# Attention scores through the leaky slope first: one exponential a graph with its row sum on ScalarE, in a four-stage graph and mixture kernel

## What is computed

```python
x = x + _L0_gnn_ref(_layernorm(x), adj, ...)      # slope 0.2,  elu at the end
x = x + _L0_ffn_ref(_layernorm(x), ...)           # 8 experts, the best two of each node
x = x + _L1_gnn_ref(_layernorm(x), adj, ...)      # slope 0.01, relu at the end
x = x + _L1_ffn_ref(_layernorm(x), ...)           # 32 experts, the best one

h = x @ W
s1, s2 = h @ a1, h @ a2
e = leaky_relu(s1[:, :, None] + s2[:, None, :], negative_slope=alpha)
attention = softmax(where(adj > 0, e, NEG_BIG), axis=-1)
h_prime = attention @ h
```

## Time and profile before

| | us |
|---|---|
| median of 3 runs | 1112.64 (1110.25 to 1114.04) |
| the profiled execution | 1112.51 |
| its span | 1110.8 |
| mean granted TensorE clock | 0.879 |

### The profile page before, as it was taken

How to read it: one execution, slowest core, us unless ns; L and a number is a source line. 1 busy time by engine, 2 the same in 40 slices (tenths; PEclk the granted TensorE clock), 3 DMA queues, 4 the chain that set the end, 5 groups by cost and what they waited for, 6 DMA issues and landing times. The chain is left out here.

```text
span 1110.8 us, 26952 instructions
## 1 busy us (share of the span) xinstructions
PE 888.1 (80%) x6709; PEld 799.2 (72%) x6709; DVE 788.0 (71%) x3507; ACT 699.1 (63%) x2364; POOL 765.7 (69%) x983
## 2 busy tenths in 40 slices
PE   5988898888619999999999669999999418888720
PEld 4777787777509999999999658888888406666620
DVE  7688989898848999999999617888888713322310
ACT  3998988898405655656656369999998216643300
POOL 4347767777753888887788801778787846777776
PEclk9998989898659999999999979999999659976655
DMA  9333442221167888877878221222221135433301
GB/s 213 69 96 118 135 133 60 64 73 33 40 141 201 210 212 211 206 210 209 207 206 208 66 68 39 79 79 79 79 81 51 53 96 145 116 99 105 93 31 38
DMA packets 144904, 129.21 MB, mean 116 GB/s; under 512 B 26521, under 2 KB 116510, under 8 KB 144754
## 3 DMA queue, kind: packets, MB, share of 16 engines
q1 hardware_dynamic: 124114, 91.94, 33.4%
q0 software_dynamic: 17760, 34.20, 9.1%
q10 hardware_dynamic: 2880, 1.35, 0.6%
HBM read 82.74 MB, written 47.48 MB: 117 GB/s over the span
## 5 line engine op out<-in xcount | busy, mean ns | idle before, releaser
L505 POOL DMA_INDIRECT xs<-staged,dst x256 | 258.8, 1011 | 77.0 <-issue 68.5
L1172 ACT ACTIVATE hT<-bank,wt 128x128 f32<-128x128 f32 x620 | 177.3, 368 | 131.3 <-PE bank L1392 115.3
L551 POOL DMA_INDIRECT x2d<-ob,xi x155 | 161.3, 1040 | 41.6 <-issue 27.3
L573 POOL DMA_INDIRECT out<-oq,xq x144 | 142.8, 991 | 58.2 <-issue 42.7
L1378 PE MATMUL bank<-xnT,wt 128*128 128x128 f32 x1240 | 165.8, 277 | 0.0
L1392 PE MATMUL bank<-w2s,hT 128*128 x1240 | 164.1, 275 | 0.6 <-DVE ob L1044 0.5
L1378 PEld LDWEIGHTS bank<-xnT,wt 128*128 128x128 f32 x1240 | 152.6, 194 | 0.1
L1392 PEld LDWEIGHTS bank<-w2s,hT 128*128 128x128 f32 x1240 | 150.9, 192 | 1.0 <-issue 1.0
L1121 ACT ACTIVATE p<-bank,nm 128x128 f32<-128x128 f32 x256 | 103.1, 403 | 19.6 <-DVE nm L746 19.6
L1122 ACT ACTIVATE p<-bank,nm 128x128 f32<-128x128 f32 x256 | 104.8, 410 | 0.0
L1135 ACT ACTIVATE rl<-bank,rinv 128x128 f32<-128x128 f32 x256 | 97.1, 453 | 3.1 <-DVE staged L738 3.1
(11 more groups left out here) (249 smaller groups left out, 2202.6 us busy)
## 6 DMA issues: line engine op xcount, KB each, us to landing
wt<-wpd SPq DMA_DIRECT2D x155, 258.0 KB
xi<-xs SPq DMA_DIRECT2D x155, 66.0 KB
xq<-xs SPq DMA_DIRECT2D x144, 66.0 KB
xb<-x2d SPq DMA_DIRECT2D x32, 258.0 KB, 3.2
xb<-in_x SPq DMA_DIRECT2D x32, 256.0 KB, 3.2
wpd<-w1c SPq DMA_DIRECT2D x56, 129.0 KB, 3.3
xs<-staged,dst POOLq DMA_INDIRECT x256, 2.6
x2d<-ob,xi POOLq DMA_INDIRECT x155
```

The lines of the kernel that those rows point to most:

```text
L505: pool.indirect_dma_start(out=xs[l], out_offset=bass.IndirectOffsetOnAxis(ap=dst[b % ND][:, c:c + 1], axis=0), in_=stag[s][:, q, 0:ROW], i ...
L551: pool.indirect_dma_start(out=x2d, out_offset=bass.IndirectOffsetOnAxis(ap=xi[t % NXI][:, ID:ID + 1].bitcast(U32), axis=0), in_=ob[:, t % ...
L573: pool.indirect_dma_start(out=orow, out_offset=bass.IndirectOffsetOnAxis(ap=xq[j % NXQ][:, q, ID:ID + 1].bitcast(U32), axis=0), in_=oq[j % ...
L1172: last = act.activation(hT[t % 2][:, j, :], HID[t % 2][:, j, :], ACT.Gelu, bias=wt[t % NW][:, c:c + 1])
```

## The change

The score is put through the leaky slope before the exponential: S + min(S, 0)(slope - 1). In layer 1 VectorE does it, with a tensor_scalar from PSUM into `leaky` and an add. In layer 0 ScalarE forms relu((slope - 1) S), which is min(S, 0)(slope - 1), into `leaky` (event `below`), and VectorE adds S. The row maximum with its sign turned is then `nm` itself. ScalarE takes one exponential a graph from `leaky`, with `accum_out` for the row sum. `pm`, `nm`, `rsum` and `leaky` have two buffers each. TensorE now waits for `leaky` of group m-2 before it forms scores, and for `exps` before the transpose of `pm`; the moments' parts stand in a row ahead of the reciprocal.

```diff
             def weights(n, moments=()):
+                for part in moments:
+                    part()
                 after(dve, "exps", n)
-                after(dve, "pt_ps", n - 1)
                 after(dve, "er", n - 3)
-                for q in range(G):
-                    last = dve.scalar_tensor_tensor(pm[:, q, :], p1[:, q, :], 0.0, p2[:, q, :], ALU.max, ALU.max,
-                                                    accum_out=rsum[:, q:q + 1])
-                    if q == 3:
-                        last.then_inc(sem("pm"), 1)
-                    if q % 2 and moments:
-                        moments[q // 2]()
-                after(dve, "pm", n)
-                dve.reciprocal(rinv[n % 3][:, :], rsum[:, :]).then_inc(sem("rinv"), 1)
+                dve.reciprocal(rinv[n % 3][:, :], rsum[n % 2][:, :]).then_inc(sem("rinv"), 1)
...
             def scores(n):
                 l = n // NG
-                after(dve, "s_ps", n)
-                after(dve, "exps", n - 1)
-                link(dve.reduce_max(nmax[:, :], g4(SB[n % 2]), AX.X, negate=True))
-                dve.scalar_tensor_tensor(nm[:, :], nmax[:, :], SLOPE[l], nmax[:, :], ALU.mult, ALU.min).then_inc(sem("nm"), 1)
+                S, L = g4(SB[n % 2]), leaky[n % 2][:, :, :]
+                if l == 0:
+                    after(dve, "below", n)
+                else:
+                    after(dve, "s_ps", n)
+                    after(dve, "exps", n - 2)
+                    link(dve.tensor_scalar(L, S, 0.0, SLOPE[l] - 1.0, ALU.min, ALU.mult))
+                dve.tensor_tensor(L, L, S, ALU.add).then_inc(sem("leaky"), 1)
+                after(dve, "leaky", n)
+                dve.reduce_max(nm[n % 2][:, :], L, AX.X, negate=True).then_inc(sem("nm"), 1)
...
                         after(act, "nm", m)
-                        after(act, "pm", m - 1)
-                        S = g4(SB[m % 2])
+                        after(act, "pt_ps", m - 2)
+                        after(act, "rinv", m - 2)
                         for q in range(G):
-                            act.activation(p1[:, q, :], S[:, q, :], ACT.Exp, bias=nm[:, q:q + 1])
-                            last = act.activation(p2[:, q, :], S[:, q, :], ACT.Exp, bias=nm[:, q:q + 1], scale=SLOPE[l])
+                            last = act.activation(pm[m % 2][:, q, :], leaky[m % 2][:, q, :], ACT.Exp, bias=nm[m % 2][:, q:q + 1],
+                                                  accum_out=rsum[m % 2][:, q:q + 1])
                         last.then_inc(sem("exps"), 1)
...
                         act.activation(x1T[:, :], XP[:, :], ACT.Copy).then_inc(sem("x1T"), 1)
+                    if l == 0 and 0 <= i - 1 < NG:
+                        m = n - 1
+                        after(act, "s_ps", m)
+                        after(act, "exps", m - 2)
+                        act.activation(leaky[m % 2][:, :, :], g4(SB[m % 2]), ACT.Relu, scale=SLOPE[l] - 1.0).then_inc(sem("below"), 1)
...
-                        after(pe, "exps", m - 2)
+                        after(pe, "leaky", m - 2)
                         S = SB[m % 2]
...
-                        after(pe, "pm", n - 2)
+                        after(pe, "exps", n - 2)
                         after(pe, "x1T", min(n - 5, l * NG + NG - 1) if i >= 5 else l * NG - 1)
-                        turn(XP, pm, "pt_ps")
+                        turn(XP, pm[n % 2], "pt_ps")
```

More of the change, by code:

```diff
@@ L186, in program @@
         nmax = sb("nmax", [P, G])
[L187 to L190, removed]
+        nm = [sb(f"nm{s}", [P, G]) for s in range(2)]
+        leaky = [sb(f"leaky{s}", [P, G, P]) for s in range(2)]
+        pm = [sb(f"pm{s}", [P, G, P]) for s in range(2)]
         pt = sb("pt", [P, T])
-        rsum = sb("rsum", [P, G])
+        rsum = [sb(f"rsum{s}", [P, G]) for s in range(2)]
         rinv = [sb(f"rinv{s}", [P, G]) for s in range(3)]
```

## The result

The changed kernel takes 1126.7 us (median of four runs, 1123.9 to 1131.3) where the kernel before takes 1112.2 (1110.3 to 1114.0) on the same chip: ratio 1.013, interval 1.010 to 1.016, some 14.5 us slower. Its profiled execution has a span of 1124.2 us for 1110.8. The forecast was 1120 with 1100 to 1130: the direction and the range hold, but the change is nearly twice the forecast one (7.5 us), and 1126.7 lies just above the 1114 to 1126 that the forecast gave itself.

The account below looks back on a forecast made before the run. First pass: loop of scores, relu, add, reduction, `residual`, `staged` turn, with matmuls late at half clock; second: GpSimd before, 13.09 us floor. 1112.5 + 6.7 + 2 - 1 = 1120.2, said as 1120; range 1100 to 1130.

Parts of the forecast that it names:

- The steady part of the first pass: Eleven pairs of steps in layer 0's attention: 190.6 us for 184.9, +5.7.
- A-steps: First-pass steps with `places`, from the score reduction after a route to the next: 6.98 us, 8.97 with a late matmul.
- B-steps: First-pass steps with the route, alternating with A-steps: 8.90 us each, for 9.35 before.
- The first steps: First five steps of the first pass, in one term with its last: relu's delay bare, 0 to 3.4 us, +2 taken.
- The last steps of the pass: First-pass pairs beyond the eleven, thirteen in all, taking the loss from +5.7 to +6.7 us.
- The second pass: Layer 1's attention: pair 13.48 us for 13.63, -2 over some 14 pairs, +1 before GpSimd starts; together -1.
- bound of -7.6: Most that the second pass could gain, in us: 0.54 a pair over 14 pairs.
- floor of 13.09: Second pass, GpSimd's lowest time for a pair: 13.63 us less its 0.54 us wait for `dst`.
- (c): Second pass comes down to GpSimd's floor as VectorE reads PSUM quicker: -7.6 us for -1, total 1114; chance 0.13.
- (a): Half clock in each A-step of the first pass: eleven pairs 196.6 us, +11.7; total 1127; chance 0.15.
- (b): Half-clock dips of the first pass vanish: pair 15.88 us, -12.1 in thirteen; total 1101; chance 0.14.
- (d): ScalarE not relieved, row sums costing 0.4 us each: +9 us in thirteen first-pass pairs; total 1129; chance 0.08.

Follow-up runs that it names:

- e4: Changed kernel with `residual` put ahead of `scores` on VectorE in both layers; 1102.6 us, ratio 0.990 to the kernel before.
- e6: Changed kernel with four idle mask matmuls on TensorE ahead of its wait for `staged`, in each B-step of the first pass's steady part; ratio 0.9985 to the kernel before.
- e9: Kernel before with four idle mask matmuls on TensorE in each B-step of the first pass's steady part; ratio 0.989 to the kernel before.
- e2: Changed kernel with only layer 0's attention in the new form, layer 1's as before; 1132.4 us, ratio 1.013 to the kernel before.
- e11: The changed kernel itself, run again on another chip; ratio 1.016 to the kernel before on that chip.
- e3: Changed kernel with layer 0's relu moved on ScalarE from ahead of the `xs_` copies to behind them; 1134.9 us, ratio 1.018 to the kernel before.
- e5: Changed kernel with the first eight groups of layer 0 taking the slope on VectorE, no relu on ScalarE for them; ratio 1.005 to the kernel before.
- e10: Changed kernel with layer 0's slope on VectorE for the whole first pass, no relu on ScalarE; ratio 1.018 to the kernel before.
- e12: Changed kernel with four idle mask matmuls in each steady B-step and three in each of steps 4 to 8; ratio 0.997 to the kernel before.
- e1: Changed kernel with only layer 1's attention in the new form, layer 0's as before; 1108.6 us, ratio 0.994 to the kernel before.
- e8: Changed kernel with exponentials left without `accum_out`, a constant standing for the row sums; ratio 1.014 to the kernel before.

## Why the prediction was right, and where its sizes were off

**The steady part of the first pass.** Worked out at 92.7 us for eleven A-steps and 97.9 for eleven B-steps. Measured: A 7.02, 9.93, 8.61, 8.61, 8.51, 9.90, 6.97, 7.02, 8.49, 8.27 and 9.85, in all 93.2; B 97.9. Three A-steps are at full clock (6.97 to 7.02 for the 6.98 given) and eight have a stretch at half clock (9.02 on average for 8.97, but 8.27 to 9.93 one by one). e4 shows the loop and e6 and e9 the clock by taking each away: the mechanism was right. That B fits to the tenth is in part luck: ten of the eleven are 8.97 on average for the 8.90 given, and the last one is 8.13. That eight of eleven should dip was taken over from the kernel before, without a reason why it should stay so, and that it did was luck: it was six in e2, the same first pass on the same chip, ten in e11 and all eleven in e3, e5 and e10. With e2's count the +5.7 would have measured +1.5.

**The first steps: the term that was mis-sized.** "Between 0 and 5 x 0.67 = 3.4, I take +2" measured +9.9 to reduction 8. I counted the relu's own delay there and forgot the sentence that I had written for the steady part, that `xs_`, `hg`, `pt` and `xT` are queued behind it and are covered only because `staged` comes later still. In the first steps no `staged` is awaited, so nothing covers them. 6.6 us of the 9.9 arise up to reduction 3, where the granted clock is 1.00 (20 to 50 us), from the closed loop alone; 3.3 in the five steps after, where it is 0.83 in three of the four windows of 10 us, and where e12 puts about 3 parts in 5 of such a loss to the clock. With e5 all but 1.1 us (85.28 for 84.20) is traced to the relu on ScalarE. This term too differs from one execution to the next: in e11 it was 14.3 against e9, with half clock in the steps to reductions 1 and 7 too (11.86 us for 10.19, 8.81 for 7.27); in e2 the step to reduction 7 was 8.81, and e4, also on the result's chip, had the 11.86.

**The last steps of the pass** give 2.0 back; I had 1.0 more lost there, at 0.5 a pair. Why they gain was not looked into. Of these 2.0, and of the 9.9 ahead, 0.7 is only the reduction's later place in its step.

**The second pass.** -1 forecast, -5.4 measured. The pair is 13.34 for the 13.48 given (7.00 + 6.34 for 7.12 + 6.36), which is -0.28 in place of -0.14, -3.3 in the twelve full pairs. The steps before GpSimd starts I had put at +1; the first seven measured -1.4 (41.5 us for 42.9): one step of 8.89 us with the first route in it became 7.00. The two ends of the pass make up the remaining -0.7. It stayed within the bound of -7.6. The pair of 13.34 is above the floor of 13.09 that rival (c) goes by, and no larger wait for `dst` is left: the loop over `staged`, for which TensorE waits in each step, holds the pair.

**The last mixture.** Nothing was forecast, and 4.8 us came: 4.0 in the stores (185.7 us from first to last, then 189.7), 0.8 in the way to the first. The code is the same. What differs is when TensorE's clock comes up (windows of the kernel before from 20 us behind its second table, then of the changed one from 24 us behind its own):

```profile
912.00:922.00 10.00, 7.86 (x47) 5.55 (x45) 2.67 (x4) 5.21 (x23) 2.16 (x3) 0.77 0.45 105
922.00:932.00 10.00, 8.35 (x61) 6.52 (x60) 3.93 (x6) 6.35 (x28) 7.56 (x8) 1.00 0.65 170
```

```profile
925.00:935.00 10.00, 9.22 (x41) 6.97 (x42) 2.00 (x4) 4.71 (x23) 3.95 (x4) 0.55 0.53 131
935.00:945.00 10.00, 8.37 (x62) 6.57 (x62) 3.95 (x7) 6.32 (x29) 6.70 (x7) 1.00 0.58 153
```

On this chip e1 and e3 have such stores too (189.6 and 189.4 us), and so has e2 (191.1), whose second pass and mixtures are those of the kernel before. e4, in which the clock rises as early as in the kernel before, has 186.9. Between e9 and e11 there is no difference. So the longer stores come without the new second pass, as in e2, and stay away with it, as in e4 and e11; they go along with a late rise of the clock. That this rise is their cause is argued from the windows and not shown, and what sets it was not tried: these 4.8 us, a third of the measured change, stay open.

**How the number came out.** The terms measured +14.0, -5.4 and +4.8 where +7.7 in all was forecast. The first two miss by +5.3 and -4.4 and nearly cancel; alone they would have given +8.6. That 1126.7 lies inside the range owes as much to this as to the mechanism.

**The rivals.** (a), half clock in every A-step, did not come in the changed kernel's profile, but nearly so in e11 and wholly in e5 (195.3 us for the 196.6 worked out). (b) did not come by itself; e6 shows its time, 174.7 us for eleven pairs as in 11 x 15.88, when the dips are taken away by force. (c) fell: tensor_scalar and add hold VectorE for the 0.73 given (starts at 669.81 and 670.54 us). (d) fell with e8.

**What the profile was to show.** A at 6.98 or about 9 (8.27 to 9.93) and B at 8.9, the relu waiting for the score matmuls, the waits for exponentials gone: all there. Of the signs of being wrong none came: A is nowhere under 6.7, the pair of the second pass is 13.34 and not 13.1, the clock of the first pass 0.87 and not 1.00, and the exponentials start 0.39 us apart and not over 0.5.

## What to carry to other kernels

Work moved to a less busy engine goes into that engine's queue, and its wait holds up all that stands behind it; walk each loop of waits once for the steady state and once again for the first steps, where the work that covers it there has not begun. Where less work makes a stage longer, ask which order in the program, not which engine, closes the loop: one exchange of two blocks on VectorE turned a loss of 1.3% into a gain of 1.0%. And where a kernel's matmul engine pauses in each step, measure once with the pause filled: it tells what the clock costs, here 13 to 16 us of stages of 185 and 191 us. A stage whose length hangs on such dips differs between executions of one kernel (186 to 191 us here on one chip), so profile it more than once before a difference of a few us is put down to a change.

## What the runs showed of the hardware

- An exponential with a row sum on ScalarE leaves a second record of 0.19 to 0.28 us behind it, and four of 128 elements start 0.39 us apart instead of 0.25. With the sum left out (e8) the four last 1.28 us together, with no second record, and the program's ratio (1.014) is not told apart from that with it.
- TensorE's granted clock stands at one of its two levels (0.50 or 1.00, so 1.2 or 2.4 GHz); in this stage it fell behind the pause of 1.4 to 1.5 us in which the engine waited for `staged`, and four idle matmuls in that pause (1.02 us together) kept every step of the steady part at 1.00, in two different kernels (e6, e9). Not each such pause brings a fall: three of eleven A-steps went without.
- Where the clock falls differs from one execution to the next for the same instructions: eight of eleven A-steps in the changed kernel and six in e2, on one chip; reduction 8 of the changed kernel came at 94.1 us on one chip and 98.3 on another, by half-clock stretches in the steps to reductions 1 and 7.
